# Graph stack in four stages: first normalisation moved ahead of the first weight rounding, and twenty transposes of the identity put first on TensorE

## The reference

```
h = relu(layernorm(x)); x = x + gnn0(h, adj)   # two rounds: m_left = h Wl', m_right = h Wr',
                                               # u = h m_left' and h m_right' by triangles,
                                               # exp(u)*adj, rows normalised, times (h W_lin' + b), layer norm, relu
h = relu(layernorm(x)); x = x + att1(h, adj)   # 12 heads: q, k, v, softmax(q k' * scale + bias), times v, Wo
h = relu(layernorm(x)); x = x + att2(h, adj)   # the same with other weights and bias
h = relu(layernorm(x)); x = x + gnn3(h, adj)   # two rounds: softmax(h h'), times adj, three projections, layer norm, relu
```

## Time and profile before

| what | value |
|---|---|
| median of 3 runs | 2811.89 us |
| the three runs | 2810.28 to 2812.11 us |
| span of the profiled execution, first to last instruction | 2807.3 us |
| TensorE busy in that span | 2738.0 us, 98% |
| VectorE busy | 2029.9 us, 72% |
| GpSimd busy | 1434.8 us, 51% |
| ScalarE busy | 1281.6 us, 46% |
| mean share of full clock that TensorE was granted | 0.994 |

### The profile page before, as it was taken

The page is one execution under the profiler, slowest core; times in us unless marked ns, Lnnn a source line. Parts: engine busy times, 40 slices in busy tenths (PEclk is TensorE's granted clock), DMA queues, the critical chain, the costliest instruction groups (busy, mean ns, idle before and its releaser), DMA issues.

```text
span 2807.3 us, 86091 instructions
## 1 busy us (share of the span) xinstructions
PE 2738.0 (98%) x34304; PEld 2536.4 (90%) x34304; DVE 2029.9 (72%) x3998; ACT 1281.6 (46%) x2069; POOL 1434.8 (51%) x2499
## 2 busy tenths in 40 slices
PE   7999999999999999999989999999999999999998
PEld 7999999999988999999989999999888888888887
DVE  4666666766687777777777777778667767776776
ACT  3334334334344444444444444444545545445443
POOL 1212212122224555555545555555777777778777
PEclk9999999999999999999999999999999999999999
DMA  4121121211112111111131111112112112111121
GB/s 155 43 78 45 56 67 41 82 41 62 62 55 84 49 49 49 49 49 49 43 101 49 49 49 49 49 49 68 39 39 75 37 42 70 37 64 48 37 75 34
DMA packets 116535, 158.88 MB, mean 57 GB/s; under 512 B 8048, under 2 KB 112368, under 8 KB 116464
## 3 DMA queue, kind: packets, MB, share of 16 engines
q1 hardware_dynamic: 116464, 157.88, 17.2%
HBM read 107.52 MB, written 50.33 MB: 56 GB/s over the span
## 4 chain that ended last, share of the span: by engine, by line
PE 52%; POOL 25%; issue 12%; DVE 5%; ACT 3%; DMA 1%; POOLq 1%; SPq 0%; DVEq 0%; ACTq 0%
PE ps L226 38%; POOL wide L1347 6%; POOL wide L933 5%; POOL wide L924 4%; PE ps L1160 3%; PE ps L786 2%; PE ps L1191 2%; POOL wide L1332 2%; PE ps L809 2%; POOL wide L1336 2%; PE ps L1177 2%; PE ps L726 2%; ACT wide L996 2%; POOL rstd L1366 1%; POOL x_rstd L891 1%
## 5 line engine op out<-in xcount | busy, mean ns | idle before, releaser
L226 PE MATMUL ps<-w_hi,split 128*128 128x384 f32 x4608 | 1269.2, 344 | 8.3 <-ACT wide L962 4.6
L226 PEld LDWEIGHTS ps<-w_hi,split 128*128 128x128 f32 x4608 | 847.5, 190 | 23.8 <-ACT wide L962 5.0
L226 PE MATMUL ps<-split,w_hi 128*128 128x256 f32 x4608 | 865.0, 283 | 1.7 <-DVE split L640 1.6
L226 PE MATMUL ps<-w_lo,split 128*128 128x384 f32 x2304 | 778.3, 338 | 1.6 <-issue 1.6
L226 PEld LDWEIGHTS ps<-split,w_hi 128*128 128x128 f32 x4608 | 724.5, 189 | 25.3 <-issue 13.8
L226 PE MATMUL ps<-split,w_lo 128*128 128x256 f32 x2304 | 575.5, 280 | 0.0
L226 PEld LDWEIGHTS ps<-w_lo,split 128*128 128x128 f32 x2304 | 436.5, 189 | 0.0
L226 PEld LDWEIGHTS ps<-split,w_lo 128*128 128x128 f32 x2304 | 435.4, 189 | 0.0
L933 POOL TENSOR_TENSOR wide<-wide 128x192 f32<-128x192 f32 x256 | 212.3, 858 | 405.3 <-ACT wide L996 405.3
L1347 POOL TENSOR_TENSOR wide<-wide,row 128x192 f32<-128x192 f32 x512 | 312.6, 645 | 29.8 <-ACT wide L1430 29.8
L514 POOL TENSOR_TENSOR rstd<-mv,pos_half 128x2 f32<-128x2 f32 x64 | 43.6, 691 | 453.4 <-DVE mv L694 453.4
(11 more groups left out here) (131 smaller groups left out, 4549.6 us busy)
## 6 DMA issues: line engine op xcount, KB each, us to landing
x_after<-wide SPq DMA_DIRECT2D x96, 384.0 KB, 2.5
xin<-x_after SPq DMA_DIRECT2D x96, 384.0 KB, 3.4
xin<-in_x SPq DMA_DIRECT2D x32, 384.0 KB, 4.1
wide<-in_x SPq DMA_DIRECT2D x32, 384.0 KB, 3.6
wide<-x_after SPq DMA_DIRECT2D x32, 384.0 KB, 4.1
out<-wide SPq DMA_DIRECT2D x32, 384.0 KB, 2.8
adjin<-in_adj SPq DMA_DIRECT2D x32, 256.0 KB, 3.6
w_raw<-in_w SPq DMA_DIRECT2D x3, 2304.0 KB, 13.7
```

The costliest lines, as they stand in the source:

```text
L226: last = nc.tensor.matmul(out, t if tokens_stay else w, w if tokens_stay else t, start=(k == 0), stop=(k == len(pairs) - 1))
```

## The change

Four edits, of which the third alters no order.

1. `split_hi` of matrix 0 no longer stands at the head of ScalarE's program. It is issued in `norm`, behind the two instructions that normalise the tokens of stream 0.
2. TensorE's first work, behind its wait for the identity, is `WARMING` = 20 transposes of the identity into the last bank of stream 1's PSUM, which nobody reads.
3. `exact_product` takes a first and a last third, and each step that is such a product can be named in the orders whole or in parts (`a`, `b`, `c` behind its name). The orders name only whole steps. In the attention stages `q`, `v` and `out` are now named by their chunks, one behind another where the one word stood.
4. Line breaks of the order strings.

```diff
+WARMING = 20
 ATT_ORDERS = [
-    "q.1' k0.1' k1.1' v.1' pt0.0' hT.0 pt1.0' pt2.0' k2.1' pv.0' scores.1' out.0' q.0 k0.0 k1.0 v.0 "
-    "pt0.1' hT.1 pt1.1' pt2.1' k2.0 pv.1' scores.0 out.1'",
+    "q0.1' q1.1' q2.1' k0.1' k1.1' v0.1' v1.1' pt0.0' hT.0 pt1.0' pt2.0' k2.1' pv.0' scores.1' out0.0' "
+    "out1.0' q0.0 q1.0 q2.0 k0.0 k1.0 v0.0 v1.0 pt0.1' hT.1 pt1.1' pt2.1' k2.0 pv.1' scores.0 out0.1' "
+    "out1.1'",
...
+PARTS = "abc"
+def parted(stages):
+    return {piece: (whole, first, last) for whole in stages for first in range(len(PARTS))
+            for last in range(first, len(PARTS))
+            for piece in {whole + PARTS[first:last + 1]} | ({whole} if last - first == len(PARTS) - 1 else set())}
+def ends(events):
+    return {piece: names for whole, names in events.items() for piece, (_, _, last) in parted([whole]).items()
+            if last == len(PARTS) - 1}
+def pieces(stages):
+    def cut(stage, first, last):
+        return lambda s, i: stage(s, i, first, last)
+    return {piece: cut(stages[whole], first, last) for piece, (whole, first, last) in parted(stages).items()}
...
-def exact_product(nc, out, terms, tokens_stay=False, tokens_lo_made=None):
+def exact_product(nc, out, terms, first, last, tokens_stay=False, tokens_lo_made=None):
...
-    for k, (w, t) in enumerate(pairs):
+    for k in range(len(terms) * first, len(terms) * (last + 1)):
+        w, t = pairs[k]
...
             ins.then_inc(act_done[s], 1)
+            if first(s, i):
+                for m in EARLY:
+                    split_hi(act, g, phases, phase, m)
...
         @block.scalar
         def _(act):
-            for m in EARLY:
-                split_hi(act, g, phases, 0, m)
             run(act, 1, lambda n, m: split_hi(act, g, phases, n, m))
...
         @block.tensor
         def _(pe):
             pe.wait_ge(g.ident_in, 16)
+            for _ in range(WARMING):
+                nc.tensor.transpose(g.ps[STREAMS - 1][:, 3, 0:P], g.ident[:], g.ident[:])
             run(pe, 0)
```

More of the change, by code:

```diff
@@ L425, in both @@
         return {f"{st}_{l}": [f"{name}_{l}" for name in names] for l in range(2) for st, names in stages_.items()}
-    PE = counts(pe_order, both({"ml2": ["ml"], "mr2": ["mr"], "lin1": ["lin"], **{n: [n] for n in ["hT", "u", "aT", "agg"]}}))
+    PE = counts(pe_order, both({**ends({"ml2": ["ml"], "mr2": ["mr"], "lin1": ["lin"]}),
+                                **{n: [n] for n in ["hT", "u", "aT", "agg"]}}))
     AC = counts(act_order, {"norm": ["h"], **both({"hT": ["hT"], "ml": ["ml"], "mr": ["mr"], "soft": ["e"],
@@ L728, in hT, with project_T @@
                 mm.then_inc(pe_done[s], 1)
-            def project_T(s, i, out, m, o):
+            def project_T(s, i, out, m, o, first, last):
                 b = bufs[s]
@@ L750, in mr, with stage @@
             def mr(o):
-                def stage(s, i):
-                    if o == 0:
+                def stage(s, i, first, last):
+                    if o == 0 and first == 0:
                         weights_made(pe, g, phase, 3 * l + RIGHT, i)
@@ L756, in stage @@
                             pe.wait_ge(act_done[s], AC[s]("z_1", i - 1))
-                    mm = project_T(s, i, bufs[s].rows[1 - l], RIGHT, o)
-                    if o == C - 1:
+                    mm = project_T(s, i, bufs[s].rows[1 - l], RIGHT, o, first, last)
+                    if o == C - 1 and last == len(PARTS) - 1:
                         mm.then_inc(pe_done[s], 1)
@@ L762, in lin, with stage @@
             def lin(t):
-                def stage(s, i):
+                def stage(s, i, first, last):
                     b = bufs[s]
-                    if t == 0:
+                    if t == 0 and first == 0:
                         weights_made(pe, g, phase, 3 * l + LIN, i)
@@ L770, in stage @@
                         (g.w_hi[:, SLOTS[phase][3 * l + LIN], c], g.w_lo[:, SLOTS[phase][3 * l + LIN], c], b.t_hi[:, c, at], b.t_lo[:, c, at])
-                        for c in range(C)], tokens_stay=True)
-                    if t == T - 1:
+                        for c in range(C)], first, last, tokens_stay=True)
+                    if t == T - 1 and last == len(PARTS) - 1:
                         mm.then_inc(pe_done[s], 1)
@@ L1098, in hT, with project_T @@
             mm.then_inc(pe_done[s], 1)
[L1100 to L1106, removed]
+        def project_T(b, out, m, o, first, last, tokens_lo_made=None):
+            return exact_product(nc, out[:, o], [
+                (g.w_hi[:, SLOTS[phase][m], c, o * P:(o + 1) * P], g.w_lo[:, SLOTS[phase][m], c, o * P:(o + 1) * P],
+                 b.t_hi[:, c], b.t_lo[:, c]) for c in range(C)],
+                first, last, tokens_lo_made=tokens_lo_made if o == 0 else None)
         def o_taken(s, i, graph):
@@ L1113, in o_taken, with q, stage, tokens_lo_made @@
                 pe.wait_ge(before.dve_done[s], before.DV[s](f"o_lo_{graph}", ITER - 1))
[L1115 to L1127, removed]
+        def q(o):
+            def stage(s, i, first, last):
+                def tokens_lo_made():
+                    pe.wait_ge(dve_done[s], DV[s]("t_lo", i))
+                if first == 0:
+                    if o == 0:
+                        pe.wait_ge(act_done[s], AC[s]("t_hi", i))
+                        o_taken(s, i, 0)
+                        weights_made(pe, g, phase, WQ, i)
+                    if o == C - 1:
+                        o_taken(s, i, 1)
+                mm = project_T(bufs[s], bufs[s].ps_row, WQ, o, first, last, tokens_lo_made=tokens_lo_made)
+                if o == C - 1 and last == len(PARTS) - 1:
+                    mm.then_inc(pe_done[s], 1)
+            return stage
+        def k(o):
+            def stage(s, i, first, last):
+                if o == 0 and first == 0:
                     pe.wait_ge(dve_done[s], DV[s]("t_lo", i))
@@ L1133, in stage, with v @@
                     weights_made(pe, g, phase, WK, i)
-                mm = project_T(bufs[s], bufs[s].ps_row2, WK, chunks=(c,))
-                if c == C - 1:
+                mm = project_T(bufs[s], bufs[s].ps_row2, WK, o, first, last)
+                if o == C - 1 and last == len(PARTS) - 1:
                     mm.then_inc(pe_done[s], 1)
             return stage
-        def v(s, i):
-            b = bufs[s]
-            pe.wait_ge(act_done[s], AC[s]("q", i))
-            weights_made(pe, g, phase, WV, i)
-            for t in range(T):
+        def v(t):
+            def stage(s, i, first, last):
+                b = bufs[s]
+                if t == 0 and first == 0:
+                    pe.wait_ge(act_done[s], AC[s]("q", i))
+                    weights_made(pe, g, phase, WV, i)
                 at = slice(t * P, (t + 1) * P)
@@ L1146, in v @@
                     (g.w_hi[:, SLOTS[phase][WV], c], g.w_lo[:, SLOTS[phase][WV], c], b.t_hi[:, c, at], b.t_lo[:, c, at])
-                    for c in range(C)], tokens_stay=True)
-            mm.then_inc(pe_done[s], 1)
+                    for c in range(C)], first, last, tokens_stay=True)
+                if t == T - 1 and last == len(PARTS) - 1:
+                    mm.then_inc(pe_done[s], 1)
+            return stage
         def scores(s, i):
@@ L1221, in tensor_stages @@
-        return todo
+                    first, last, tokens_stay=True, tokens_lo_made=tokens_lo_made if t == 0 else None)
+                if t == T - 1 and last == len(PARTS) - 1:
+                    mm.then_inc(pe_done[s], 1)
+            return stage
+        return {"hT": hT, "scores": scores, "pv": pv, **{f"pt{c}": pt(c) for c in range(C)},
+                **pieces({**{f"q{o}": q(o) for o in range(C)}, **{f"k{o}": k(o) for o in range(C)},
+                          **{f"v{t}": v(t) for t in range(T)}, **{f"out{t}": out(t) for t in range(T)}})}
@@ L1618, in hT, with project @@
                 mm.then_inc(pe_done[s], 1)
-            def project(b, t, bank, m, tokens_lo_made=None):
+            def project(b, t, bank, m, first, last, tokens_lo_made=None):
                 if m == ON:
```

116 lines of the change are left out of this document (62 added, 54 removed), and 42 rows, old and new, of the table BETWEEN.

## The result

The changed kernel takes 2817.1 us in the median of 8 runs (2815.17 to 2821.75), against 2811.73 us for the kernel before in 8 runs beside it. The ratio is 1.0024, with a 95% interval of 1.0014 to 1.0034, so it is slower: by 5.4 us between the medians, and by 4 to 10 us by the interval. Its time lies outside the forecast range of 2807.5 to 2813.9. One run of the kernel before took 10943.9 us and is left out of the ratio.

What follows compares the result with a forecast made beforehand. TensorE was taken to bound the first stage's loop, but the start also waits on other engines and the parameter load. Terms -0.42 + 0.17 - 1.45 = -1.70 us took 2811.89 to 2810.2 us; range 2807.5 to 2813.9.

Steps and rivals of the forecast that it cites:

- The sooner weight transfer: At the start, matrices 4 and 5 are issued some 1.9 us sooner; cost taken as 0, with 0.95 us kept for the range.
- Rival (a): At the start, the transposes don't raise TensorE's clock; only -0.42 us is gained, 2811.5 us; chance 0.30.
- The low clock after the long idle time: TensorE idles 4.2 us before `u`, so its clock is low from about 23 us for some 3.4 us.
- the bound taken for `u`: The 48 small matmuls of `u` at the low clock: between 0 and +1.24 us, taken as 0.
- The term of +0.17: Stream 1's transposes at the low clock take +0.63 us, of which 0.46 is covered by ScalarE's copy: +0.17 us.
- -0.42: At the start, `u` comes at 23.53 instead of 23.95 us, as ScalarE normalises stream 1 before copying `ml`: -0.42 us.
- The low stretch ahead of `agg`: Idle time before `agg` shrinks from 2.23 to about 0.7 us, so the clock stays high there: -1.45 us, bounds 0 and -1.5.
- A changed loop: Example of something no forecast or rival has, left outside the range: 0.03 on the fast side, 0.03 on the slow.
- (b): At the start, the twenty transposes don't overlap and take 426 ns each, `u` at 24.9: +1.0 us, 2812.9 us; chance 0.06.
- (c): The low clock after the idle time lasts into the products behind `agg`: -0.25 and about +0.75 us, 2812.4 us; chance 0.09.
- Rival (d): Other low-clock stretches, as at 1400 to 1450 us, fall differently by 1.5 us and hide the gain: 2810.4 to 2813.4; chance 0.10.

Runs made afterwards that it cites:

- first pair of traces: Traces of the first runs of the changed kernel (2817.1 us) and the kernel before (2811.73 us); ratio 1.0024.
- second pair: Traces of both kernels run once more, unchanged: the changed kernel 2818.97 us, the kernel before 2810.39 us.
- a shift of 256: Changed kernel plus a never-executed branch over 217 instructions ahead of TensorE's wait for the identity, moving later code by 256 instructions: 2811.95 us, ratio 1.0004.
- before again: The kernel before, run once more with nothing changed: 2810.39 us, ratio 1.0004.

## Why the prediction was wrong

- **Edit 1, moment by moment: right.** Normalisation 7.07 (forecast 7.13), real transposes 8.54 (8.6), first product 11.43 (11.7), ScalarE's wait for matrix 2 until 13.33 (13.5), statistics of stream 1 at 18.45, released by `ln_cols` (18.4), normalisation of stream 1 at 21.37 (21.3), `u` at 23.42 (23.5). That `u` came within 0.1 us is luck in part, as its spread above is 0.7 us. The first product's time is made of other parts than forecast: six real transposes of 0.82 us and not 1.51, then 2.07 us to the first product and not 1.60. The 2 us gained ahead of the first product don't get past the parameter load. The sooner weight transfer wasn't tried by itself; the kernel without the transposes, which contains it, bounds its cost with the rest of edit 1 at 0.14%.
- **Edit 2, as work: right.** Twenty transposes took 4.44 us (4.4) and lay beside the wait for the tokens.
- **Rival (a), and the Trainium skill's sentence behind it** ("TensorE: Matmul & The Clock Gate", Part 4, PE-mode transpose): against the trace. The transposes did raise the clock. Behind them the six real ones take 0.82 us where they took 1.51, and the first products are 0.12 us apart where they were 0.21. The kernel without transposes has its six in 1.51 us. But the gain was short: after the first four products came the low stretch from 11.9 to 15.3 us, which the forecast of 45 products at 0.12 us didn't have. They ended at 19.9 instead of 19.3, and as `u` had to wait for the parameters anyway, nothing hung on it.
- **The low clock after the long idle time: right in kind, wrong in size.** TensorE stood idle for 3.49 us ahead of `u`, and the granted clock was low behind it. By windows (columns as in rows 1):

```profile
22.00:26.00 4.00, 2.58 (x51) 2.30 (x52) 0.36 (x1) 1.37 (x3) 3.05 (x8) 0.52 0.07 26
26.00:30.00 4.00, 4.00 (x18) 3.97 (x18) 2.82 (x6) 3.20 (x5) 0.00 (x0) 0.63 0.00 0
```

  The stretch was twice as long as forecast, from 22.1 to 28.9 us (0.63 over the four microseconds from 26 is low for 3 of them), and the bound taken for `u` was the wrong one: its 48 small matmuls took 2.15 us and not 1.24, so +0.9 and not 0. The term of +0.17 was about +1.2 (34.30 for `agg`, where -0.42 alone would have made 33.1). The kernel without transposes has such a stretch as well: 3.57 us of idle time, then 2.15 us for `u`. So rival (a), which had the clock stay up there, was wrong in that too.
- **The low stretch ahead of `agg`: right.** It didn't come, 0.88 us instead of 1.56. The start's three terms then sum to -0.42 + 1.2 - 1.45 = -0.7 us where the forecast had -1.70, and -0.7 is what the first pair of traces shows at 40 us. The second pair shows +0.3, so even the sign isn't certain.
- **The step that failed.** It is the costing of edit 2 by its execution alone, with the sentence that follows from it, that nothing outside the first microseconds changes. Twenty transposes are also 39 instructions at the head of a program of which one stretch after another is fetched in blocks of 256, and at two seams, 800 and 1400 us later, they moved a fetch's boundary into the small matmuls. That cost 5.4 us at the two seams in the first pair of traces, where the forecast had zero. In the prediction this stood nowhere: neither as a term nor as a rival. "A changed loop" was named as what is left outside, at 0.03; it was the code between the loops.
- **Rivals (b) and (c)**, the two slower ones, didn't happen: the transposes overlapped, and the clock was high at `agg`. Both had the side right, slower, but neither reason was at work. Rival (d) named the windows of the second seam, but by their clock. The low stretches of the two seams add up to 20.5 us before, 23.9 us after, and 23.9 us in the kernel without transposes too, so they don't tell the slow kernel from the fast ones.
- **It could have been read before.** In the kernel before, the page's queue part lists the 51 instruction packets, and the seam's timeline has the 1.96 us pause in the middle of a run of one line's matmuls, where no other engine is waited for. (The 12% that the page's chain gives to "issue" is no such sign: it is over 300 us, and the pauses in `scores` are 7.1.)

The Trainium skill, "Advanced Engine Details and Errata", ISA Cache, says that an engine's instructions are cached in lines of 16 KB, 256 instructions, and that TensorE has room for 128 KB of them. The runs agree on the line: packets of 16 KB, pauses that lie whole multiples of 256 instructions apart, and a shift of 256 that restores the time where 39 costs 0.24 to 0.35%. On the room they only show that the attention stage's loop runs without pauses of this kind: between 945 and 1375 us TensorE's only waits are 2.8 us for GpSimd, in both kernels, and from 980 to 1380 us before a single packet of the 51 is fetched.

What stays open is what starts a fetch, and so why it starts so late: in most of these pauses the packet started 0.2 to 1.1 us before TensorE ran dry, in some only after it. Open too is why TensorE goes on only 1.2 to 1.6 us behind the packet's end, and what the 1.4 us behind 2100 us are in the first pair. Nor was it tried to write the seams so that `scores` lies inside a block, which is where a gain would be: the pauses in `scores` alone are 6.4 to 7.1 us in the kernel before.

## What to carry to other kernels

An instruction has a price at its place in the program as well as on its engine. Where an engine's program is long, written out in part and full of very short instructions, ask of each added instruction what it shifts, and look in the trace for pauses marked issue in the middle of a run of one line's work. To tell such a layout effect from the effect of the work, add the same number of instructions that do nothing, and then fill up to a whole block: if the first reproduces the loss and the second takes it away, the work was never the cause.

## What the runs showed of the hardware

- TensorE's instructions are fetched in blocks of 256 (pauses 512, 768 and 1280 instructions apart, packets of 16 KB). TensorE can pass into a block 2.2 to 3.0 us after its packet started. A block that isn't there in time costs a pause of up to 3.1 us, mostly of 1.5 to 2.3. The places are the same in every execution of a program; whether a pause falls there is not: the same boundary cost 0, 0.41 and 1.74 us in three traces with the same layout (before, before again, without transposes).
- Transposes of the identity alone raised TensorE's clock: the six transposes behind twenty of them took 0.82 and 0.87 us in the two traces of the changed kernel, and 1.51 us without them. Behind the same twenty in a hardware loop, 0.39 us apart, they took 1.52 us. After 2.07 us of idle time and four products the clock was low again, for 3.4 us.
- Twenty transposes take 4.44 us in a row and 7.92 us in a hardware loop of one.
- A burst of 48 small matmuls of 96 columns takes 1.20 us at the high clock and 2.15 us at the low one, so the clock counts for it in nearly full measure.
- A wait that is already met, carried by an instruction that does nothing, takes TensorE 0.11 us (40 of them from 4.5 to 8.8 us).
